# Six of eight batches' transposed activations kept whole and split later, and the transfer of the row maxima moved ahead of a store

## The chip, the cores and the metric

One Trainium2 chip, one of its cores. The metric is the device time of one execution in microseconds (us). The kernel is launched once; everything below happens inside that launch.

## What is computed

The input is `x`, 8 batches of 512 tokens of 256 numbers. After a layer norm over the 256 numbers (`xn`), three things are added:

    x + attention(xn) + moe(xn) + shared_mlp(xn)

- **Attention.** q, k and v come from low-rank projections (`xn @ basis.T`, 32 wide, then `@ (amp*cos(phase)).T`), 16 heads of 16; softmax over 512 keys; then another low-rank projection.
- **MoE.** Logits `xn @ gate_w.T` for 8 experts, softmax, the two best per token, and for these `silu(x@w_gate)*(x@w_up) @ w_down` with F = 352.
- **Shared MLP.** The same form with a hidden width of 704, for every token.

The kernel keeps float32 accuracy out of faster matmuls: an operand is split in a high part (rounded to the type the text below calls f32r) and a low part (the rest), and three products HI*HI, LO*HI, HI*LO are summed. A matmul of two whole float32 operands needs no split.

## The kernel before, in words

**Early part (to about 93 us).** VectorE (DVE) measures each batch (`measure`, L1660) and works out its scale (`scales`, L1672) with one square root on ScalarE (`root`, L870). ScalarE writes three quarters of the normed rows (`normal`, L875), GpSimd (POOL) one quarter. TensorE (PE) turns the rows (`turn_rows`, L1175), ScalarE copies the result rounded (`columns_high`, L884: two 128x512 copies) and DVE subtracts to get the low part (`columns_low`, L1721: two 128x512 subtractions). PE makes the logits (`logits`, L1184: four matmuls of 512 columns, high and low part of the activations against a gate whose 16 columns hold its own high and low part). The sync engine (SP) stores the rows for the experts' gather and both parts of the columns (`store_columns`, L482: 1 MB a batch) for the late part. Each engine runs its list in the order in which the code calls these helpers (ScalarE L897 to L918, PE L1201 to L1212, DVE L1731 to L1747). Routing follows on DVE from L1756.

**Middle part (93 to 367 us).** 71 tiles of 128 gathered tokens go through their experts (L1277 to L1341). Only the batch loads for the late part lie in it.

**Late part (367 to 950 us).** Batches are taken in reverse: batch b of this part is batch 7-b of the input (`of`, L398). Each batch has four slots g = 0 to 3, one per group of four heads, and each slot eight steps t = 0 to 7. In a step PE makes transposed scores (`score_T`), scores of a later group for the maxima (`score`), products with the values (`values`, float32 on both sides) and a piece of the shared MLP; ScalarE takes one exponential of 128x1024 (`exponent`, L1077), DVE one maximum of 128x1024 (L1872). The order on every engine is written out by hand (`slot` of ScalarE at L1109, of PE at L1600, of DVE at L1941, of SP at L662).

The maxima of group g+1 are made ready in slot g: DVE splits them at step 3 (`split_max`, L1874, two tiny operations from SBUF to SBUF), PE turns them at step 4 (L1383), ScalarE copies them at step 5 (`max_rows`, L1038), SP moves them into two rows of q (`load_max`, L631). The first `score_T` of the next slot waits for that transfer.

SP's other work in a slot: storing q's and k's parts of the next batch (`store_qk`, L620: three DMAs of 256 KB each, numbers 0 and 1 in slot 0, numbers 2 and 3 in slot 1), loading them back per group (`load_rows`, L548: four DMAs of 192 KB), moving the heads' sums and values (`move_sums` L637, `move_values` L643), and, for the heads of slots 2 and 3 of the batch before, storing the inverse sums (`store_inverse`, L651, in slot 0) and reading them back spread over the partitions (`load_inverse`, L656, in slot 1). POOL multiplies with these (`normalise`, L790), ScalarE rounds the product at step 4 of slot 1 (`ao_high`, L1092, L1095), ahead of `max_rows` in its list, POOL takes the low part (`ao_low`, L796), and PE uses both at step 7 of slot 1 (`low_rank_o`, L1551). `load_xT` (L585) brings the columns of batch b+2 (1 MB) in slot 2; PE's `low_rank(b+2)` (L1457) reads them at step 2 of slot 3.

## Time and profile before

| | us |
|---|---|
| median of 3 runs | 949.67 (949.47, 949.67, 953.66) |
| the profiled execution, its own time | 951.79 |
| its span in the profile | 950.0 |
| PE busy in the span | 864.2 (91%) |
| DVE busy | 612.4 (64%) |
| ScalarE busy | 574.5 (60%) |
| GpSimd busy | 410.4 (43%) |
| DMA moved | 140.04 MB |

A row of a timeline has a start, a duration, the engine, the line of the kernel, the operation, what it writes and reads, a count, and in brackets the idle time of that engine ahead of it with what ended it. PEld is the load of weights into PE. SPq rows are DMA issues: the duration is that of the issue and not of the transfer. A whole float32 matmul shows as two records.

### The profile page before, as it was taken

The numbers are of one execution on the slowest core, as the hardware profiler recorded it, in microseconds if no ns is written. First come the engines' busy times: TensorE is split into PE (matmuls) and PEld (weight loads), VectorE is DVE, ScalarE is ACT, GpSimd is POOL, SyncE is SP. The second block draws the span as 40 slices with busy tenths as digits, with TensorE's granted clock in tenths as the row PEclk, the third lists the DMA queues.
The fourth block names the chain that finished last, engine by engine and source line by source line (L and its number), as shares of the span: only waits on it lengthen the run. The fifth ranks groups of instructions, "written<-read, shape, count | busy, mean of one in ns | idle before, by whom it ended". The sixth has DMA issues, their size and how long they took to land.

```text
span 950.0 us, 19558 instructions
## 1 busy us (share of the span) xinstructions
PE 864.2 (91%) x6491; PEld 604.9 (64%) x6492; DVE 612.4 (64%) x923; ACT 574.5 (60%) x935; POOL 410.4 (43%) x411
## 2 busy tenths in 40 slices
PE   4755999999999989889989999999989999989995
PEld 2435999999999986456546555555546555555552
DVE  7787843434344455776776776776776786777752
ACT  5746744444444442766766866866756766767754
POOL 2003622222222151752762762753752763763841
PEclk9875999999999999989999999999999999999998
DMA  9994656222222216553863764754754865755410
GB/s 306 391 292 142 217 142 181 69 72 72 69 75 66 66 46 169 165 169 90 208 184 100 202 190 115 200 178 119 195 177 111 202 181 123 189 137 112 104 48 24
DMA packets 91480, 140.04 MB, mean 147 GB/s; under 512 B 17512, under 2 KB 51824, under 8 KB 89488
## 3 DMA queue, kind: packets, MB, share of 16 engines
q1 hardware_dynamic: 84720, 121.24, 44.7%
q0 software_dynamic: 6480, 17.70, 7.1%
q8 instruction: 44, 0.72, 0.3%
q14 instruction: 28, 0.23, 0.1%
q10 hardware_dynamic: 208, 0.14, 0.1%
HBM read 79.24 MB, written 54.71 MB: 141 GB/s over the span
## 4 chain that ended last, share of the span: by engine, by line
PE 68%; DVE 15%; DMA 6%; issue 4%; ACT 3%; SPq 2%; POOL 2%; DVEq 0%; ACTq 0%; POOLq 0%
PE s_pair L1295 8%; PE bank L1313 8%; PE bank L1453 8%; PE bank L1413 8%; PE bank L1517 7%; PE s_pair L1366 7%; PE st_pair L1295 6%; DVE top L1872 6%; PE st_pair L1441 5%; PE bank L1303 2%; PE bank L1278 2%; DMA q_rows<-top_T 1%; PE bank L1466 1%; DVE stats L1664 1%; PE bank L1426 1%
## 5 line engine op out<-in xcount | busy, mean ns | idle before, releaser
L1872 DVE TENSOR_REDUCE top<-s_pair 128x2 f32<-128x1024 f32 x248 | 303.7, 1224 | 139.6 <-PE s_pair L1366 138.2
L1083 ACT ACTIVATE prob<-st_pair 128x1024 f32<-128x1024 f32 x252 | 258.6, 1026 | 130.1 <-PE st_pair L1441 126.5
L756 POOL DMA_INDIRECT xg<-xn_rows,token_of x71 | 81.1, 1142 | 209.8 <-PE bank L1278 159.0
L1453 PE MATMUL bank<-prob,v_ones 128*32 128x512 f32 x1024 | 138.0, 611 | 2.2 <-ACT prob L1083 2.1
L1366 PE MATMUL s_pair<-k_rows,q_rows 48*128 48x512 f32 x496 | 113.4, 448 | 17.3 <-DVE top L1872 16.3
L1413 PE MATMUL bank<-xT_b,w_sh 64*128 64x512 f32 x960 | 128.8, 400 | 0.2
L1441 PE MATMUL st_pair<-q_rows,k_rows 50*128 50x512 f32 x504 | 105.5, 411 | 5.8 <-DMA q_rows<-top_T 3.0
L1413 PEld LDWEIGHTS bank<-xT_b,w_sh 64*128 64x128 f32 x960 | 90.3, 187 | 24.0 <-DVE h_f L1887 2.2
L1313 PE MATMUL bank<-w_exp,c_hT 128*128 (+1 forms) x639 | 94.2, 292 | 0.6 <-ACT c_y L995 0.6
L1366 PEld LDWEIGHTS s_pair<-k_rows,q_rows 48*128 48x128 f32 x496 | 48.1, 186 | 64.1 <-DVE top L1872 49.1
L1295 PE MATMUL s_pair<-w_exp,xg_T 128*128 x468 | 88.1, 338 | 0.0
L794 POOL TENSOR_TENSOR ao<-ao,o_sum 128x512 f32<-128x512 f32 x15 | 19.3, 1285 | 149.7 <-DMA o_sum<-inverse_rows 149.7
L1517 PEld LDWEIGHTS bank<-w_sh,h_T 64*128 64x128 f32 x1088 | 73.9, 189 | 12.5 <-issue 7.6
L1313 PEld LDWEIGHTS bank<-w_exp,c_hT 128*128 128x128 f32 (+1 forms) x639 | 81.1, 190 | 1.1 <-issue 1.1
L1517 PE MATMUL bank<-w_sh,h_T 64*128 64x256 f32 x1088 | 79.1, 286 | 2.4 <-DVE ro L1939 1.9
L778 POOL TENSOR_TENSOR h_f<-h_f,u_half 128x512 f32<-128x512 f32 x40 | 51.7, 1293 | 64.3 <-DVE h_f L1887 64.0
L1295 PEld LDWEIGHTS s_pair<-w_exp,xg_T 128*128 128x128 f32 x468 | 77.4, 195 | 0.3
L990 ACT ACTIVATE c_hT<-bank 128x384 fp32r<-128x384 f32 x71 | 34.9, 491 | 59.1 <-PE bank L1303 59.1
L1295 PE MATMUL st_pair<-w_exp,xg_T 128*128 x384 | 70.4, 332 | 0.0
L803 POOL DMA_INDIRECT y_b<-expert_rows,slot_of x64 | 63.8, 997 | 11.6 <-issue 6.6
L810 POOL TENSOR_SCALAR y_b<-y_b,share 128x256 f32<-128x256 f32 x64 | 58.4, 922 | 18.3 <-DMA y_b<-expert_rows,slot_of 18.2
L1844 DVE TENSOR_TENSOR xg_T<-bank,xg_T 128x256 fp32r<-128x256 f32 x71 | 30.1, 424 | 55.4 <-ACT xg_T L980 55.4
(230 smaller groups left out, 1229.0 us busy)
## 6 DMA issues: line engine op xcount, KB each, us to landing
qk_rows<-qk_hi SPq DMA_DIRECT2D x56, 256.0 KB
q_rows<-qk_rows SPq DMA_DIRECT2D x64, 192.0 KB
k_rows<-qk_rows SPq DMA_DIRECT2D x56, 192.0 KB
expert_rows<-c_y SPq DMA_DIRECT2D x71, 128.0 KB, 1.7
xn_T_split<-x_T SPq DMA_DIRECT2D x8, 1024.0 KB, 6.5
xT_b<-xn_T_split SPq DMA_DIRECT2D x7, 1024.0 KB, 8.7
qk_rows<-qk_lo SPq DMA_DIRECT2D x28, 256.0 KB
x_all<-in_L_attn_x_dram SPq DMA_DIRECT2D x8, 512.0 KB, 8.2
```

The source lines that it names most:

```text
L756: pool.indirect_dma_start(xg[s % 4][:, :], None, xn_dram, bass.IndirectOffsetOnAxis(token_of[:, s:s + 1], 0)).then_inc(c_x[s % 4], 16)
L803: pool.indirect_dma_start(y_b[:, t % 2, k, :], None, y_dram, bass.IndirectOffsetOnAxis(slot_of[:, k, of(b) * TPB + t:of(b) * TPB + t + 1], ...
L810: pool.tensor_scalar(y_b[:, t % 2, k, :], y_b[:, t % 2, k, :], share[:, of(b) * TPB + t, k:k + 1], None, ALU.mult).then_inc(p_ys, 1)
L1083: act.activation(prob[n % 3][:, 2 * jp:2 * jp + 2, :].rearrange("p j l -> p (j l)"), score_T_pair(b, g, t)[:, :], ACT.Exp, scale=HD ** -0. ...
L1295: ins = pe.matmul(gu_bank_of(s, i)[n][:, 0:F], xg_T[i % 2][:, a * KT + k, :], w, start=(m == 0 and k == 0), stop=(m == 2 and k == KT - 1))
L1313: ins = pe.matmul(y_bank[:, 0:D], c_hT[i % 2][0:n, a, k, :], w, start=(m == 0 and k == 0), stop=(m == 2 and k == FT - 1))
L1366: ins = pe.matmul(score_pair(b, g, v)[:, i * 512:(i + 1) * 512], q_rows[g][r:r + 48, jp, qt * P:(qt + 1) * P], k_rows[g][r:r + 48, jp, :], ...
L1413: ins = pe.matmul((g_bank, u_bank)[up][:, :], w_sh[rows, a, o:o + P], xT_of(b)[rows, c, k, :], start=(n == 0 and i == 0), stop=(n == 1 and ...
L1441: ins = pe.matmul(score_T_pair(b, g, t)[:, i * 512:(i + 1) * 512], k_rows[g][r:r + QK_ROWS, jp, kt * P:(kt + 1) * P], q_rows[g][r:r + QK_R ...
L1453: ins = pe.matmul(ot_bank[32 * j:32 * j + 32, :], v_ones[:, kt, 4 * g + j, :], prob[(b * 16 + g * 4 + kt) % 3][:, j, :], start=(kt == 0), ...
L1517: ins = pe.matmul((g_bank, u_bank)[to][:, 0:D], h_T[rows, a, f, t * P:(t + 1) * P], w_sh[rows, c, S_GU + f * D:S_GU + (f + 1) * D], start= ...
L1872: dve.tensor_reduce(top[g % 2][:, :, jp, qt], score_pair(b, g, v)[:, :].rearrange("p (i k) -> p i k", i=2), AX_X, ALU.max).then_inc(d_max, 1)
```

## The change

1. Batches 0 to 5 of the input (`in_parts` false) are kept as whole float32 columns: ScalarE's two copies write float32, DVE's two subtractions are left out, PE makes the logits with two float32 matmuls instead of four, and SP stores 512 KB instead of 1 MB. PE's `turn_rows` waits for the copy of two batches before, no longer for its subtraction. DVE adds one memset and two copies of 128x8 for a float32 gate.
2. In the late part `load_xT` reads 512 KB for these batches (b = 2 to 7 there). ScalarE makes the high part in one copy of 128x1024 (`columns_out`, slot 2, step 6), POOL the low part in one subtraction of 128x1024 (`columns_rest`, ahead of `last_group`). PE waits for POOL's `p_xl`.
3. In SP's list of a slot `load_max` is ahead of `store_qk` 0 and 2, and `load_xT` is behind `load_inverse`, `move_sums` and `move_values`.
4. Two semaphores are merged into others (`rows_ok` into `hot_ok`, `d_iv` into `d_to`), with the same waits.

```diff
@@ SP
+        WHOLE = NB - 2
+        def in_parts(b):
+            return b >= WHOLE
...
             def store_columns(b):
                 wait(sp, xt_hi, b + 1)
-                wait(sp, xt_lo, b + 1)
+                if not in_parts(b):
+                    sp.dma_start(xT_dram[b][:, 0:KT * L],
+                                 x_W[b % NXT][:, HI, :, :].rearrange("p k l -> p (k l)")).then_inc(xT_stored[b % NXT], 16)
+                    return
+                wait(sp, xt_lo, b - WHOLE + 1)
...
             def load_xT(b):
                 if b >= 2:
                     wait(sp, b_gu, (b - 1) * SFT)
+                if in_parts(of(b)):
...
+                else:
+                    sp.dma_start(xT_of(b)[:, LO, :, :].rearrange("p k l -> p (k l)").bitcast(F32), xT_dram[of(b)][:, 0:KT * L]).then_inc(xT_in, 16)
...
             def slot(b, g):
-                if g == 2 and there(b + 2):
-                    load_xT(b + 2)
                 if ppg % 2 and moved(ppb, ppg // 2):
                     load_inverse(ppb, ppg // 2)
                 if pg % 2 and moved(pb, pg // 2):
                     move_sums(pb, pg)
                     move_values(pb, pg)
-                if g == 0 and there(b + 1):
-                    store_qk(b + 1, 0)
-                if g == 1 and there(b + 1):
-                    store_qk(b + 1, 2)
+                if g == 2 and there(b + 2):
+                    load_xT(b + 2)
                 if g == 2 and there(b - 1):
                     store_out(b - 1, 0)
                 if g == 3 and there(b + 2):
                     store_low_rank(b + 2)
                 if there(nb):
                     load_max(nb, ng)
+                if g == 0 and there(b + 1):
+                    store_qk(b + 1, 0)
+                if g == 1 and there(b + 1):
+                    store_qk(b + 1, 2)
@@ GpSimd
+            def columns_rest(b):
+                wait(pool, a_xh, b - 1)
+                lo = xT_of(b)[:, LO, :, :].rearrange("p k l -> p (k l)")
+                pool.tensor_tensor(lo, lo.bitcast(F32), xT_of(b)[:, HI, :, :].rearrange("p k l -> p (k l)").bitcast(F32),
+                                   ALU.subtract).then_inc(p_xl, 1)
...
                 sum_y(b, 3)
+                if there(b + 2):
+                    columns_rest(b + 2)
                 last_group(b)
@@ ScalarE
-                    ins = act.activation(x_T[b % NXT][:, HI, k, :], xt_bank[b % 2][k][:, :], ACT.Copy)
+                    ins = act.activation((x_T if in_parts(b) else x_W)[b % NXT][:, HI, k, :], xt_bank[b % 2][k][:, :], ACT.Copy)
...
+            def columns_out(b):
+                wait(act, xT_in, b * 16)
+                act.activation(xT_of(b)[:, HI, :, :].rearrange("p k l -> p (k l)"),
+                               xT_of(b)[:, LO, :, :].rearrange("p k l -> p (k l)").bitcast(F32), ACT.Copy).then_inc(a_xh, 1)
...
+                    if g == 2 and t == 6 and there(b + 2):
+                        columns_out(b + 2)
@@ TensorE
-                wait(pe, xt_lo, b - 1)
+                wait(pe, xt_hi, b - 1)
...
             def logits(b):
-                wait(pe, xt_lo, b + 1)
                 wait(pe, lg_kept, b)
+                if not in_parts(b):
+                    wait(pe, xt_hi, b + 1)
+                    for k in range(KT):
+                        ins = pe.matmul(lgT_bank[0:2 * NE, :], gate_F[:, k, :, :].rearrange("p c e -> p (c e)"), x_W[b % NXT][:, HI, k, :],
+                                        start=(k == 0), stop=(k == KT - 1))
+                    ins.then_inc(lg_turned, 1)
+                    return
+                wait(pe, xt_lo, b - WHOLE + 1)
...
             def low_rank(b):
-                wait(pe, xT_in, b * 16)
+                wait(pe, xT_in, 16) if b == 1 else wait(pe, p_xl, b - 1)
@@ VectorE
             small_parts()
-            columns_low(0)
             scales(2)
             for b in range(3, 7):
                 measure(b)
-                columns_low(b - 2)
                 scales(b)
-            columns_low(5)
             angles()
-            columns_low(6)
-            columns_low(7)
+            for b in range(WHOLE, NB):
+                columns_low(b)
             thrice()
```

## Rows read from the trace of the kernel before

**Rows 1.** Busy time by engine, granted clock and DMA, of the late part.

```profile
core 0: us, PE busy (x) PEld busy (x) DVE busy (x) ACT busy (x) POOL busy (x), PEclk, DMA share, GB/s
...
367.40:950.00 582.60, 545.11 (x4395) 310.50 (x4395) 412.09 (x487) 390.32 (x532) 310.12 (x302) 0.98 0.56 147
```

**Rows 2.** Waits by releaser: us in total, times, longest.

```profile
PEld st_pair L1441 <- DMA q_rows<-top_T: 6.6, 6, 2.2
...
PE st_pair L1441 <- DMA q_rows<-top_T: 3.0, 2, 1.7
```

**Rows 3.** Chain that ended last, early part: start, us, what.

```profile
15.30 1.17 DVE x_T L1724 x2
...
32.83 1.19 DVE x_T L1724 x2
...
46.31 0.70 DVE lg L1756
```

**Rows 4.** Timeline of ScalarE, early part.

```profile
25.72 1.57 ACT L881 ACTIVATE x_n<-x_all,rs 128x256 f32<-128x256 f32 x3
...
29.44 1.57 ACT L881 ACTIVATE x_n<-x_all,rs 128x256 f32<-128x256 f32 x3
...
34.96 1.58 ACT L881 ACTIVATE x_n<-x_all,rs 128x256 f32<-128x256 f32 x3 [0.92 <-DVE rs L1679]
```

**Rows 5.** Timeline of PE, early part: the logits of two batches.

```profile
34.07 1.89 PE L1190 MATMUL bank<-x_T,gate_T 128*16 128x512 f32 x4 [1.56 <-DVE x_T L1724]
...
41.84 1.11 PE L1190 MATMUL bank<-x_T,gate_T 128*16 128x512 f32 x4
```

**Rows 6.** Timeline of PE, end of slot 1 of batch b = 3.

```profile
621.19 0.40 PE L1441 MATMUL st_pair<-q_rows,k_rows 50*128 50x512 f32 x2
621.52 1.06 PE L1453 MATMUL bank<-prob,v_ones 128*32 128x512 f32 x8
...
626.95 0.50 PE L1441 MATMUL st_pair<-q_rows,k_rows 50*128 50x512 f32 x2 [1.69 <-DMA q_rows<-top_T]
...
627.75 1.93 PE L1453 MATMUL bank<-prob,v_ones 128*32 128x512 f32 x8
```

**Rows 7.** Busy time by engine of five batch periods, columns as in rows 1.

```profile
651.52:724.05 72.53, 68.76 (x554) 39.14 (x550) 54.03 (x63) 48.63 (x68) 38.62 (x38) 0.98 0.60 161
724.05:793.74 69.69, 67.15 (x554) 38.33 (x550) 52.92 (x63) 49.16 (x68) 39.95 (x39) 1.00 0.64 168
sum 354.06, PE 339.07 PEld 193.23 DVE 263.58 ACT 244.57 POOL 195.79; mean PE 67.81 PEld 38.65 DVE 52.72 ACT 48.91 POOL 39.16
```

**Rows 8.** Timeline of SP, slots 0 and 1 of batch b = 3.

```profile
599.14 1.36 SPq L627 DMA_DIRECT2D qk_rows<-qk_hi  x2
...
606.40 0.35 SPq L654 DMA_DIRECT2D inverse_rows<-o_inv  x1
...
611.11 0.62 SPq L660 DMA_DIRECT2D o_sum<-inverse_rows  x1
...
619.45 1.82 SPq L634 DMA_DIRECT2D q_rows<-top_T  x2
```

**Rows 9.** Timeline of GpSimd, slots 2 and 3 of b = 2, slot 1 of b = 3.

```profile
579.84 1.28 POOL L794 TENSOR_TENSOR ao<-ao,o_sum 128x512 f32<-128x512 f32 x1 [17.09 <-DMA o_sum<-inverse_rows]
...
616.87 1.29 POOL L794 TENSOR_TENSOR ao<-ao,o_sum 128x512 f32<-128x512 f32 x1 [0.28 <-DMA o_sum<-inverse_rows]
```

**Rows 10.** Timeline of ScalarE, slot 1 of batch b = 3.

```profile
618.65 0.65 ACT L1095 ACTIVATE ao_T<-ao 128x512 fp32r<-128x512 f32 x1
...
619.38 1.03 ACT L1083 ACTIVATE prob<-st_pair 128x1024 f32<-128x1024 f32 x1
```

**Rows 11.** Timeline of ScalarE, step 7 of slot 2 of batch b = 2.

```profile
573.50 1.02 ACT L1083 ACTIVATE prob<-st_pair 128x1024 f32<-128x1024 f32 x1 [1.61 <-PE st_pair L1441]
```

**Rows 12.** Single lines of code: durations in ns, least, median, most; last row: landing of load_xT.

```profile
L764 POOL TENSOR_TENSOR w_sh<-raw_all,w_sh x4: 2494/2520/2547, 338.2 to 351.8; 128x1088 fp32r<-128x1088 f32 x4
...
L1881 DVE TENSOR_TENSOR top_parts<-top,top_parts x32: 174/176/1345, 366.4 to 916.4; 128x16 fp32r<-128x16 f32 x32
...
DMA to landing us min/median/max: 5.4/8.7/9.0
```

More of the change, by code:

```diff
@@ L137, in build_program @@
         gate_T = sb("gate_T", [P, KT, 2, NE], F32R, region)
+        gate_F = sb("gate_F", [P, KT, 2, NE], F32, region)
         stats = sb("stats", [P, NT, 6], F32, region)
@@ L201, in build_program @@
         tail.close()
+        whole = ExitStack()
+        sb("first_experts_w", [P, NE - 5, 2, W_ALL], F32R, whole)
+        sb("fourth_w", [P, 2 * W_ALL], F32R, whole)
+        sb("fifth_w", [P, 2 * W_ALL], F32R, whole)
+        x_W3 = sb("x_W3", [P, 2, KT, L], F32, whole)
+        sb("rest_of_sixth_w", [P, 2 * W_ALL - 2 * KT * L], F32R, whole)
+        sb("x_n_w", [P, 2, TPB, D], F32, whole)
+        x_W = [sb(f"x_W{i}", [P, 2, KT, L], F32, whole) for i in range(3)] + [x_W3]
+        whole.close()
         e_hi += [x_T[0][:, HI, k, :] for k in range(KT)]
@@ L275, in build_program @@
         xT_stored = [sem(f"xT_stored{i}") for i in range(NXT)]
-        angle_ok, thrice_ok, rows_hi, rows_ok, norm_ok = (sem(n) for n in ("angle_ok", "thrice_ok", "rows_hi", "rows_ok", "norm_ok"))
+        angle_ok, thrice_ok, rows_hi, norm_ok = (sem(n) for n in ("angle_ok", "thrice_ok", "rows_hi", "norm_ok"))
         xt_ps = sem("xt_ps")
@@ L289, in build_program @@
         a_done = sem("a_done")
+        a_xh, p_xl = sem("a_xh"), sem("p_xl")
         c_x = [sem(f"c_x{i}") for i in range(4)]
@@ L340, in build_program @@
             sem(f"d_{n}") for n in ("r", "qk", "max", "mh", "m", "ga", "hb", "inv", "res", "dn", "po"))
-        b_to, b_bo, d_iv, d_to, a_bo, d_bo = (sem(n) for n in ("b_to", "b_bo", "d_iv", "d_to", "a_bo", "d_bo"))
+        b_to, b_bo, d_to, a_bo, d_bo = (sem(n) for n in ("b_to", "b_bo", "d_to", "a_bo", "d_bo"))
         d_hl = sem("d_hl")
@@ L1259, in _ @@
             pe.matmul(bank[1][:, 0:NT * NE], ones_b[:, :], hb, start=True, stop=True).then_inc(count_ps, 1)
-            pe.wait_ge(rows_ok, 1)
+            pe.wait_ge(hot_ok, 2)
             for n in range(3):
@@ L1399, in gate_up_shared @@
                     if q == 0:
-                        wait(pe, xT_in, b * 16) if b else wait(pe, xF_in, 64)
+                        if b >= 2:
+                            wait(pe, p_xl, b - 1)
+                        else:
+                            wait(pe, xT_in, 16) if b else wait(pe, xF_in, 64)
                         wait(pe, d_dn, b * TPB)
@@ L1544, in low_rank_o @@
                     wait(pe, p_ao, 2 * b + 1)
-                    pe.wait_ge(d_to, 1)
+                    pe.wait_ge(d_to, 2)
                 else:
@@ L1563, in turn_back @@
             def turn_back(h):
-                wait(pe, d_to, h + 1)
+                wait(pe, d_to, 2 * h + 2)
                 wait(pe, d_po, LAST * 2)
@@ L1691, in small_parts @@
             def small_parts():
+                st.did(dve.memset(gate_F[:, :, LO, :], 0.0))
                 dve.wait_ge(pe_prep, 1)
@@ L1698, in small_parts @@
                     st.did(dve.tensor_copy(basis_T[:, k, HI, 3:6, :], o))
+                    st.did(dve.tensor_copy(gate_F[:, k, HI, :], g))
                     st.then(dve.tensor_copy(gate_T[:, k, HI, :], g))
@@ L1718, in small_rows @@
                                             w_rows[32:64, 2 * i:2 * i + 2, :].rearrange("p n d -> p (n d)").bitcast(F32), ALU.subtract)
[L1719 removed]
+                ins.then_inc(hot_ok, 1)
             def columns_low(b):
@@ L1925, in share_last_o @@
                 wait(dve, inv_st, (2 * LAST + 1) * 16)
-                dve.reciprocal(inv, turned_o(h)[:, :, :, HD:HD + 1]).then_inc(d_iv, 1)
-                wait(dve, d_iv, h + 1)
+                dve.reciprocal(inv, turned_o(h)[:, :, :, HD:HD + 1]).then_inc(d_to, 1)
+                wait(dve, d_to, 2 * h + 1)
                 wait(dve, p_nm, 2 * LAST + 1)
```

3 lines of the change are left out of this document (1 added, 2 removed).

## The prediction, made before the changed kernel was built or run

> **What bounds the kernel now.** I read the busy shares by stage first, then the waits by releaser, then the chain that ended last, and at the end the timelines where a wait recurs. PE is busy for 545.11 of the late part's 582.60 us [rows 1], so there only a gap on PE can be won back. One such gap belongs to the change: the first transposed scores of a slot wait for the transfer of the maxima, 3.0 us on PE in two places and 6.6 us on its weight loads in six [rows 2]. In the early part PE is not the bound. The chain runs on DVE and passes through its subtractions for the low parts, five pairs of which lie on it, the first at 15.30, the last at 32.83, 1.2 us each [rows 3]. The middle part is not touched.
>
> The five batch periods that lie wholly in the late part sum to 354.06 us, 70.81 on average; the shortest is 69.69 and the longest 72.53 [rows 7]. The shortest still does all the work, so what the others have above it, 1.1 us on average, is stall that can go.
>
> **Early part, DVE's subtractions gone.** By DVE's own list the five pairs would give 5 x 1.19 = 5.9 us. I don't take that, because ScalarE is about as late. Its normed rows start at 25.72 and 29.44, 3.72 apart, without a wait for DVE [rows 4]; that loop (turn on PE, copy, normal) stays as long as it was. Only the last one, at 34.96, waits for DVE (0.92 us), after the double measurement of batches 6 and 7 [rows 4]. By my step through the lists DVE would be done with that at 33.5 instead of 34.94, since its start hangs on ScalarE's root and not on its own list. So 1.3 us come from there. DVE's added memset and two tiny copies (some 0.1 us each, estimated from operations of that size) are inside that slack.
>
> **Early part, logits.** Four matmuls take 1.11 us at the higher clock and 1.89 at the lower [rows 5]. The price of a whole float32 matmul of 512 columns I take from the products with the values: eight records, two to a matmul, four matmuls side by side in the array, so two records one after the other, take 1.06 us [rows 6], and 1.93 when PE had just waited 1.69 us and ran at the lower of its two levels [rows 6]. Two such matmuls one after the other are 2.1 or 3.9 us: 1.0 to 2.0 us more on PE for each of six batches. PE has room for it in the loop of 3.72 us (transposes 1.1, small ones 0.4, logits 2.1: 3.6, just so) if the clock is up; at the lower clock it is 6.4 and PE would be the bound. PE did run at the lower level at 34.07, after a wait of 1.56 [rows 5]; with longer matmuls and shorter waits I expect the upper level there, which gives back another 0.5 us before the routing starts at 46.31 [rows 3]. Sum for the early part: -1.8 us, bounds -5.9 (DVE's list alone) and +3 (two batches' logits at the lower clock on the chain, 2 x 1.9, less some 0.8 won on DVE).
>
> 3 MB less are stored (6 x 0.5). Nobody on the chain waits for these stores, so they are counted at nothing; if they were what hides, the gain would be larger and not smaller.
>
> **Late part, the split.** ScalarE gains one copy of 128x1024, about 1.05 us (as an exponential of the same size, 1.02 [rows 11]), after the exponential of step 6 in slot 2. ScalarE then idles 1.61 us ahead of step 7's [rows 11], so it costs nothing if the data are there. They should be: load_xT is moved behind the five moves of sums and values and is delayed by another 2.0 us of issues in slot 1, to about 565.4 in batch 2 against 559.05; 1 MB took 8.7 us to land [rows 12], half of it should take about 6, so 571.5, and the copy would start at 571.9. That is tight. Bounds: 0, and 1 us in each of six batches. I take 0, as the row before step 7 has room for a copy that is half a microsecond late.
>
> POOL gains a subtraction of 128x1024; 128x1088 took 2.52 [rows 12], so 2.4 us. POOL idles 17.09 us there, until 579.84 [rows 9], and PE's low_rank wants it at 580.5: started at 573.0 it is done at 575.4. Cost nothing, cover 5 us. This subtraction has a second price. The two tiny operations that split the maxima take 0.18 us as a rule, but one of 32 took 1.345 [rows 12], in the longest period [rows 7], beside a POOL multiplication from SBUF. The Trainium skill, page "SBUF — State Buffer", section "SBUF: two separate sides", says that POOL and DVE share a pair of ports with an exclusive lock, so that the later one is blocked for the whole instruction. This trace agrees, with that 1.345; by the rule a subtraction of 2.4 us that met DVE's split would cost up to 2.2 us, which is rival 3. In the order as written the split is at step 3 and the subtraction after step 6, so I take 0.
>
> **Late part, SP's order.** The maxima are issued when ScalarE has copied them, at 619.45 [rows 8], and land for PE at 626.95, after 1.69 us of PE idle [rows 6]; ahead of them in the queue lie 768 KB of store_qk. At the late part's rate (147 GB/s at a DMA share of 0.56 [rows 1], so about 262 at full share) these are 3.0 us of transfer. Without them the maxima land some 3 us earlier and PE doesn't wait. Besides, PE runs at the lower level after such a wait (1.93 against 1.06 [rows 6]), another 0.9. So a stalled batch falls back to the shortest period. Batch 0 has the same gap in its slot 1 and no inverse sums to wait for: -1.3.
>
> What is late next: the three stores of q's part (1.36 for two [rows 8], so 2.0 us) now stand ahead of load_rows, store_inverse and store_qk 1. store_inverse, at 606.40, is issued some 1.7 to 2.0 later, and load_inverse, which waits for its landing (611.11 [rows 8]), with it. The product on POOL at 616.87 already waits 0.28 for that [rows 9]. It ends at 618.16, and ScalarE takes it at 618.65 [rows 10], so the first 0.5 us are free. The exponential behind it ends at 620.41 [rows 10], PE wants it at 621.19 [rows 6], so another 0.8 are free. If o_sum is later by X, PE stalls by X - 1.25. X has the bounds 0 (the same bytes in front of it in the end) and 5.0 (2.0 of issue and the 3.0 of transfer). I take 1.9, nearest to the delay of the issue: 0.65 us for each of six batches. The lateness at low_rank_o behind it should vanish in the wait of PE for DVE that follows.
>
> So a period becomes 69.7 + 0.65 = 70.35, 0.46 less than the mean before, times five: -2.3. The sixth batch: -0.5. Batch 0: -1.3. Late part: -4.1.
>
> **The sum.** -1.8 - 4.1 = -5.9 us. The profiled execution took 951.79 by its own time (span 950.0), so it would take 945.9; it stands 2.1 above the median of 949.67, and the median would be 943.8. Half a percent is 4.75 us, about what a measurement of this kernel can tell from no change.
>
> **Rivals.**
> 1. *Hidden anyway* (chance 0.20). PE's float32 logits at the lower clock take the early gain, and the end of a stalled slot is held by DVE's maxima a moment later than by the transfer, as it is in the periods without that stall. For it: the 69.69 period has no gap for the maxima and still isn't free of others. Against: the period of 70.99 with the 1.69 gap is just 1.3 longer. Then only batch 0 gains something, -0.7: 949.0.
> 2. *The inverse sums turn into the new wait* (0.14), the case on the other side. Place: ScalarE's copy of the product at step 4 of slot 1, in front of the maxima's copy and an exponential. Its price is X - 1.25 in six batches. Against 1.1 of stall that goes and the 3.6 us won elsewhere (0.6 a batch) it decides from X = 2.95. With X = 4.0, six times (2.75 - 1.1) = +9.9, less 1.3 and 1.8: +6.8, 956.5. For it: no slack on the POOL product. Against: the bytes ahead are the same in sum, and store_qk 1 will be nearly done when load_inverse is issued.
> 3. *The half megabyte lands late* (0.06). ScalarE then stands in front of step 7, POOL's subtraction slides towards the split of the maxima and can lock DVE. 1.5 us in six batches, +9.0 on the forecast: 952.8, up to 958 if the lock is met each time.
>
> **Numbers.** Forecast 0.60, own range 940 to 947, three quarters of it below 944.9; rivals 0.20, 0.14, 0.06. Faster by over half a percent: 0.45. Within: 0.15 from the forecast, 0.20 from rival 1, 0.04 from the lower ends of 2 and 3: 0.39. Slower: 0.16. The range of 8 in 10 goes from 939 (the forecast with a larger share of DVE's 5.9) to 955 (short of rival 2's value).
>
> **What would show it.** Right: routing (L1756) starts near 44.5; ScalarE's normed rows still 3.7 apart; no wait of L1441 for the maxima; ScalarE's L1095 idle by about 1.4 ahead of it; POOL's L794 in slot 1 with a wait near 2; periods near 70.3. Wrong: logits of 3.9 us in the early part; periods above 71.5 with ScalarE waiting at L1095; an idle of ScalarE ahead of columns_out; L1879 or L1881 blocked in several batches.

## The result, and the profile after

The changed kernel takes 981.68 us (median of four runs, 976.1 to 982.18) against 949.57 for the kernel before, measured beside it: a ratio of 1.032, interval 1.027 to 1.037. It is 32 us slower. The forecast was 943.8, the range ended at 955, and slower had a chance of 0.16. The profiled execution took 981.74 by its own time, with a span of 979.9. One run of e10 (979.13 us) and one of the kernel before beside e1 to e4 (961.94) fell in a slower state of the chip and are left out of the ratios.

Line numbers after the change: L818 is the product (`normalise`), L1132 ScalarE's rounding of it (`ao_high`), L1490 `score_T`, L1120 the exponential, L1412 the scores for the maxima, L1600 `low_rank_o`, L1920 DVE's maxima, L684 and L678 the load and the store of the inverse sums, L658 the maxima's transfer, L651 and L653 `store_qk`, L579 `load_rows`.

The late part, and the batch periods, from the busy time by engine (stretch, length, busy time and instructions of each engine, granted clock, DMA share, GB/s):

```profile
364.78:979.90 615.12, 563.42 (x4395) 316.16 (x4395) 410.06 (x487) 396.30 (x538) 323.16 (x308) 0.95 0.50 134
...
437.18:512.93 75.75, 70.42 (x555) 39.38 (x551) 52.48 (x63) 49.88 (x69) 41.65 (x40) 0.95 0.55 147
512.93:589.27 76.34, 71.65 (x555) 39.82 (x551) 52.00 (x63) 50.05 (x69) 41.15 (x40) 0.93 0.53 146
...
sum 378.64, PE 353.15 PEld 197.87 DVE 261.56 ACT 249.68 POOL 206.49; mean PE 70.63 PEld 39.57 DVE 52.31 ACT 49.94 POOL 41.30
```

The late part starts 2.6 us earlier than before [rows 1] and takes 32.5 us more. A period that was 70.8 on average [rows 7] is 75.7, and the granted clock, 0.98 to 1.00 before, is 0.93 to 0.95. The instructions are the same in number.

Waits by releaser (us in total, times, longest):

```profile
PEld st_pair L1490 <- ACT prob L1120: 27.5, 28, 4.9
...
ACT ao_T L1132 <- POOL ao L818: 25.9, 6, 5.7
PE st_pair L1490 <- ACT prob L1120: 23.3, 8, 4.6
```

The wait for the maxima's transfer [rows 2] is gone. In its place ScalarE waits 25.9 us in six batches for the product on POOL, which it never did before, and PE waits for ScalarE. The issues of the sync engine (SP), slots 0 and 1 of b = 3, to be laid beside [rows 8]:

```profile
611.44 1.40 SPq L658 DMA_DIRECT2D q_rows<-top_T  x2
612.95 1.32 SPq L651 DMA_DIRECT2D qk_rows<-qk_hi  x2
614.31 0.57 SPq L653 DMA_DIRECT2D qk_rows<-qk_lo  x1
614.99 2.58 SPq L579 DMA_DIRECT2D k_rows<-qk_rows  x2
617.61 1.02 SPq L579 DMA_DIRECT2D q_rows<-qk_rows  x2
618.73 0.38 SPq L678 DMA_DIRECT2D inverse_rows<-o_inv  x1
619.22 1.21 SPq L651 DMA_DIRECT2D qk_rows<-qk_hi  x2
...
624.56 0.65 SPq L684 DMA_DIRECT2D o_sum<-inverse_rows  x1
```

And two issues of the kernel before that [rows 8] leave out, between the maxima's and the store of the inverse sums:

```profile
604.23 0.80 SPq L558 DMA_DIRECT2D k_rows<-qk_rows  x2
605.06 0.91 SPq L558 DMA_DIRECT2D q_rows<-qk_rows  x2
```

POOL, ScalarE and PE behind it, from three timelines (start, us, what, in brackets the idle time ahead and its releaser; before: [rows 9], [rows 10], [rows 6]):

```profile
630.74 1.26 POOL L818 TENSOR_TENSOR ao<-ao,o_sum 128x512 f32<-128x512 f32 x1 [6.91 <-DMA o_sum<-inverse_rows]
...
632.04 0.63 ACT L1132 ACTIVATE ao_T<-ao 128x512 fp32r<-128x512 f32 x1 [4.05 <-POOL ao L818]
...
632.73 1.00 ACT L1120 ACTIVATE prob<-st_pair 128x1024 f32<-128x1024 f32 x1
...
633.78 0.49 PE L1490 MATMUL st_pair<-q_rows,k_rows 50*128 50x512 f32 x2 [3.23 <-ACT prob L1120]
634.20 1.09 PE L1502 MATMUL bank<-prob,v_ones 128*32 128x512 f32 x8
635.22 0.80 PE L1402 MATMUL bank<-r_rows,w_rows 96*128 96x512 f32 x1
...
637.10 2.87 PE L1600 MATMUL bank<-ao_T,basis_T 128*96 128x512 f32 x6
...
641.05 1.48 PE L1502 MATMUL bank<-prob,v_ones 128*32 128x512 f32 x8
```

The load of the inverse sums is issued 13.1 us behind the maxima of slot 0; before it was 8.4 (602.72 to 611.11 in the same list). The product starts 19.3 us behind them instead of 14.1. ScalarE, whose list has the rounding first, keeps the maxima's copy and the next exponential back, PE idles 3.23 us, and for some 7 us behind that its matmuls are long: 2.87 us for the six of L1600 that took 1.64 before, at the lower of the clock's two levels.

Where the DMA engines were meanwhile shows best in stretches of 4 us counted from the issue of the maxima (602.72 before, 611.44 after). Before:

```profile
596.72:600.72 4.00, 4.00 (x33) 2.07 (x29) 2.97 (x5) 3.20 (x5) 2.41 (x3) 1.00 1.10 234
600.72:604.72 4.00, 3.81 (x31) 2.06 (x29) 3.66 (x5) 3.00 (x5) 3.69 (x5) 1.00 0.61 190
604.72:608.72 4.00, 4.00 (x33) 2.11 (x29) 2.98 (x3) 3.14 (x5) 2.85 (x4) 1.00 0.96 254
608.72:612.72 4.00, 4.00 (x34) 2.42 (x32) 3.11 (x4) 3.72 (x7) 3.84 (x5) 1.00 0.66 191
612.72:616.72 4.00, 4.00 (x33) 2.22 (x31) 2.75 (x5) 3.19 (x5) 3.55 (x4) 1.00 0.49 173
```

After:

```profile
605.44:609.44 4.00, 4.00 (x33) 2.07 (x29) 2.96 (x4) 3.19 (x5) 2.90 (x4) 1.00 1.05 236
609.44:613.44 4.00, 3.34 (x28) 1.62 (x27) 4.00 (x6) 3.00 (x5) 3.73 (x5) 1.00 0.05 13
613.44:617.44 4.00, 4.00 (x33) 2.17 (x29) 2.63 (x4) 2.65 (x4) 3.71 (x5) 1.00 0.57 157
617.44:621.44 4.00, 4.00 (x34) 2.35 (x32) 3.44 (x4) 3.72 (x6) 3.75 (x5) 1.00 0.92 240
621.44:625.44 4.00, 4.00 (x33) 2.15 (x31) 2.51 (x3) 3.19 (x5) 2.23 (x2) 1.00 0.61 205
```

In the second stretch the DMA engines moved 190 GB/s before and 13 after, a difference of 177 x 4.00 = 708 KB, nearly the 768 KB of q's store. SP's last issue before the maxima ended at 607.39, and then it stood at them until 611.44. The data of q's store were ready meanwhile, the high part (512 KB) from 607.79 on and the low part (256 KB) from 610.37 on, from the timelines of ScalarE and DVE:

```profile
607.19 0.60 ACT L1068 ACTIVATE qk_hi<-bank 128x512 fp32r<-128x512 f32 x1 [0.33 <-PE bank L1402]
...
609.69 0.68 DVE L1913 TENSOR_TENSOR qk_lo<-bank,qk_hi 128x512 fp32r<-128x512 f32 x1
```

SP stood, and the DMA engines stood too. In the third stretch they are behind once more (157 GB/s against 254). In the fourth and fifth, where the inverse sums have to pass, they move more than before (240 and 205 against 191 and 173).

The early part, timelines of PE and ScalarE (before: [rows 5], [rows 4]):

```profile
23.26 1.89 PE L1229 MATMUL bank<-x_W,gate_F 128*16 128x512 f32 x4
...
26.99 1.89 PE L1229 MATMUL bank<-x_W,gate_F 128*16 128x512 f32 x4
...
23.99 1.58 ACT L913 ACTIVATE x_n<-x_all,rs 128x256 f32<-128x256 f32 x3
...
27.72 1.57 ACT L913 ACTIVATE x_n<-x_all,rs 128x256 f32<-128x256 f32 x3
```

The chain that ended last has the start of the routing (before: [rows 3]):

```profile
42.68 0.70 DVE lg L1804
```

It is 3.6 us earlier. One of these comes back at the start of the middle part, where PE waits 2.33 us for the fourth tile's gather; before it waited 0.50 there.

### The profile page after: what moved, and what is told of

Its sections match the earlier page's. It is cut to its first block, busy times and chain, and to the rows that moved or that the text cites. A ratio compares the mean times of both kernels' runs of the same rounds, so it can differ in the third digit from the quotient of the medians.

```text
span 979.9 us, 19555 instructions
## 1 busy us (share of the span) xinstructions
PE 882.6 (90%) x6491; PEld 607.7 (62%) x6492; DVE 604.6 (62%) x914; ACT 580.4 (59%) x941; POOL 424.0 (43%) x417
## 4 chain that ended last, share of the span: by engine, by line
PE 64%; DVE 11%; DMA 9%; ACT 5%; issue 5%; SPq 4%; POOL 2%; ACTq 0%; DVEq 0%; POOLq 0%
PE bank L1359 8%; PE s_pair L1341 7%; PE bank L1566 7%; PE bank L1502 7%; PE st_pair L1341 6%; PE bank L1462 6%; PE s_pair L1412 5%; DVE top L1920 5%; PE st_pair L1490 5%; DMA o_sum<-inverse_rows 3%; DMA inverse_rows<-o_inv 3%; PE bank L1349 2%; PE bank L1600 2%; SPq L579 2%; PE bank L1324 2%
## 5 line engine op out<-in xcount | busy, mean ns | idle before, releaser
L1920 DVE TENSOR_REDUCE top<-s_pair 128x2 f32<-128x1024 f32 x248 | 303.8, 1225 | 172.5 <-PE s_pair L1412 164.3
L1120 ACT ACTIVATE prob<-st_pair 128x1024 f32<-128x1024 f32 x252 | 258.5, 1026 | 127.9 <-PE st_pair L1490 118.0
L1502 PE MATMUL bank<-prob,v_ones 128*32 128x512 f32 x1024 | 141.7, 627 | 2.2 <-ACT prob L1120 2.1
L1490 PE MATMUL st_pair<-q_rows,k_rows 50*128 50x512 f32 x504 | 109.1, 425 | 23.3 <-ACT prob L1120 23.3
L1412 PE MATMUL s_pair<-k_rows,q_rows 48*128 48x512 f32 x496 | 115.4, 457 | 13.7 <-DVE top L1920 12.4
L1412 PEld LDWEIGHTS s_pair<-k_rows,q_rows 48*128 48x128 f32 x496 | 49.1, 191 | 62.0 <-DVE top L1920 45.7
L1566 PEld LDWEIGHTS bank<-w_sh,h_T 64*128 64x128 f32 x1088 | 73.7, 188 | 14.7 <-issue 9.7
L1490 PEld LDWEIGHTS st_pair<-q_rows,k_rows 50*128 50x128 f32 x504 | 50.6, 193 | 40.9 <-ACT prob L1120 27.5
L818 POOL TENSOR_TENSOR ao<-ao,o_sum 128x512 f32<-128x512 f32 x15 | 19.1, 1276 | 104.6 <-DMA o_sum<-inverse_rows 104.6
```

The lines of the kernel that those rows point to most:

```text
L1120: act.activation(prob[n % 3][:, 2 * jp:2 * jp + 2, :].rearrange("p j l -> p (j l)"), score_T_pair(b, g, t)[:, :], ACT.Exp, scale=HD ** -0. ...
L1412: ins = pe.matmul(score_pair(b, g, v)[:, i * 512:(i + 1) * 512], q_rows[g][r:r + 48, jp, qt * P:(qt + 1) * P], k_rows[g][r:r + 48, jp, :], ...
L1490: ins = pe.matmul(score_T_pair(b, g, t)[:, i * 512:(i + 1) * 512], k_rows[g][r:r + QK_ROWS, jp, kt * P:(kt + 1) * P], q_rows[g][r:r + QK_R ...
L1502: ins = pe.matmul(ot_bank[32 * j:32 * j + 32, :], v_ones[:, kt, 4 * g + j, :], prob[(b * 16 + g * 4 + kt) % 3][:, j, :], start=(kt == 0), ...
L1566: ins = pe.matmul((g_bank, u_bank)[to][:, 0:D], h_T[rows, a, f, t * P:(t + 1) * P], w_sh[rows, c, S_GU + f * D:S_GU + (f + 1) * D], start= ...
L1920: dve.tensor_reduce(top[g % 2][:, :, jp, qt], score_pair(b, g, v)[:, :].rearrange("p (i k) -> p i k", i=2), AX_X, ALU.max).then_inc(d_max, 1)
```

## The experiments

Three theories stood at first: **A**, the late inverse sums, behind the store of q's part; **B**, the split in the late part; **C**, in e1 to e4, is the new order of slot 1. A' (from e5 on) is A with the bytes between the maxima and the load of the inverse sums in the place of the store's position. From e8 on the letter C stands for the theory of volume, A' carried further: what counts is how much the DMA engines still have to move there. The groups of runs e1 to e4, e5 to e7, e8 to e10 and e11 and e12 each have their own runs of the kernel before beside them (950.13, 949.37, 950.12 and 948.48 us), so two medians of different groups compare to a us or two; the ratios are safer. All kernels compute the whole output.

**e1, the stores first again.** `store_qk` 0 and 2 back ahead of `load_max`; split and `load_xT` as changed.

```diff
+                if g == 0 and there(b + 1):
+                    store_qk(b + 1, 0)
+                if g == 1 and there(b + 1):
+                    store_qk(b + 1, 2)
                 if there(nb):
                     load_max(nb, ng)
-                if g == 0 and there(b + 1):
...
```

> The changed kernel with the maxima's transfer put back behind the stores of q's parts in slots 0 and 1; all else as changed. Theory A (the late inverse sums: in slot 0 the store of q's part now stands ahead of the rows' loads and of the store of the inverse sums, the product on GpSimd comes late, ScalarE waits for it in front of the maxima's copy, PE stalls and falls to its lower clock): 944 to 949 us, ScalarE's waits ahead of L1132 (25.9 us in the changed kernel) gone. Theory B (the split in the late part and the moved load of the columns cost the time): still 975 or more. Theory C (slot 1's new order is at fault) can't be told from A here: 944 to 949.

Measured: 945.31 us (10 runs), ratio 0.996 (0.993 to 0.999). The whole loss goes. Five periods of it:

```profile
sum 350.09, PE 336.33 PEld 191.99 DVE 262.54 ACT 249.44 POOL 209.09; mean PE 67.27 PEld 38.40 DVE 52.51 ACT 49.89 POOL 41.82
```

The changed kernel's five take 28.6 us more, 5.7 a batch. PE's busy time for the same work is 353.15 against 336.33, so 3.4 of the 5.7 us a batch are matmuls that run longer and 2.3 are idle time.

**e2, the kernel before with that order alone.** Only `load_max` ahead of `store_qk` 0 and 2.

```diff
@@ the kernel before
+                if there(nb):
+                    load_max(nb, ng)
                 if g == 0 and there(b + 1):
                     store_qk(b + 1, 0)
...
```

> The kernel before with nothing changed but the place of the maxima's transfer, ahead of the stores of q's parts in slots 0 and 1. Theory A: slower by about what the changed kernel lost plus what its early part won, 977 to 985 us, with ScalarE waiting at L1095 for 4 us in each of six batches. Theory B: 948 to 951. Theory C: as A.

Measured: 982.87 us (4 runs), ratio 1.034 (1.028 to 1.041). The order alone makes the loss, and B (the split) has no part in it.

**e3, slot 1 only.** The changed kernel with `store_qk` 0 back ahead of the maxima, number 2 still behind them.

```diff
+                if g == 0 and there(b + 1):
+                    store_qk(b + 1, 0)
                 if there(nb):
                     load_max(nb, ng)
-                if g == 0 and there(b + 1):
-                    store_qk(b + 1, 0)
```

> The changed kernel with the maxima ahead of the store in slot 1 alone; in slot 0 the store is back ahead of them. Theory A: no late inverse sums, and the maxima are early where PE had waited for them: 940 to 946 us, 2 to 5 below the run with both stores first. Theory C: 970 or more. Theory B: 975 or more.

Measured: 946.43 us (10 runs), ratio 0.996 (0.993 to 0.999). The loss comes from slot 0. In slot 1, where the maxima's transfer was the wait to be removed, the wait is gone and nothing is gained (mean of the six periods 70.73, against 70.18 in e1 and 70.67 in e7). The theory's second half, 2 to 5 us below e1, was a miss: it is 1.1 above. PE idles at that place for DVE's maximum,

```profile
626.61 0.50 PE L1412 MATMUL s_pair<-k_rows,q_rows 48*128 48x512 f32 x2 [1.02 <-DVE top L1920]
```

In e1, with the store still ahead of the maxima, PE has the same 1.02 us for DVE's maximum in three of the six slots, and itself waits for the transfer once, 0.36 us. So there was next to nothing to gain.

**e4, the store of the inverse sums early.** `store_inverse` right behind `load_max` in the changed kernel.

```diff
                 if there(nb):
                     load_max(nb, ng)
+                if pg % 2 and moved(pb, pg // 2):
+                    store_inverse(pb, pg // 2)
...
-                if pg % 2 and moved(pb, pg // 2):
-                    store_inverse(pb, pg // 2)
```

> The changed kernel with the store of the inverse sums right behind the maxima's transfer, ahead of the store of q's part and of the rows' loads. Theory A: the sums are on their way some 6 us earlier, the product on GpSimd is no longer late and the whole loss is gone: 938 to 945 us, ScalarE's waits ahead of its copy of the product under 1 us a batch. Theories B and C: 972 or more.

Measured: 989.82 us (4 runs), ratio 1.041 (1.035 to 1.048). A miss. The store goes out 5.8 us sooner (2.0 behind the maxima instead of 7.8, means over the six batches), and yet the product is later:

```profile
634.40 1.26 POOL L818 TENSOR_TENSOR ao<-ao,o_sum 128x512 f32<-128x512 f32 x1 [7.11 <-DMA o_sum<-inverse_rows]
```

That is 19.8 us behind the maxima (614.56); in the changed kernel it was 19.3. So the place of the store in SP's list isn't what decides, and A fell in that form. A' put the backlog of bytes in its place.

**e5, the inverse sums' round trip ahead of the rows.** Slot 0: maxima, `store_inverse`, `store_qk` 0 and 1, `load_inverse`, `load_rows`.

```diff
                 if there(nb):
                     load_max(nb, ng)
+                if g == 0 and moved(b - 1, 1):
+                    store_inverse(b - 1, 1)
                 if g == 0 and there(b + 1):
                     store_qk(b + 1, 0)
...
+                if g == 0 and there(b + 1):
+                    store_qk(b + 1, 1)
+                if g == 0 and moved(b - 1, 1):
+                    load_inverse(b - 1, 1)
```

> The changed kernel with slot 0 of SP in the order maxima, store_inverse, store_qk 0, store_qk 1, load_inverse, load_rows (slots 1 to 3 as changed). Nothing is left out. Theory A' (what decides is how much lies in SP's list and queue between the maxima and load_inverse): load_inverse is issued 7.1 us behind the maxima's issue instead of 13.1 (10.4 in the kernel where only store_inverse was early), POOL's product comes out 2 us before ScalarE wants it, ScalarE waits for it 0 to 3 us in all, periods of 69.7 to 70.7, 938 to 945 us. Rival E (any order with the maxima ahead of the stores delays the same bytes, and the loss only moves to k's part or to the rows of the next group): above 965 us, with the waits of e4 or new ones for k_rows. Rival B (the split in the late part): 975 us or more.

Measured: 1006.92 us (6 runs), ratio 1.060 (1.057 to 1.063). The worst of all; A' missed here, and rival E was right.

```profile
629.74 1.45 SPq L684 DMA_DIRECT2D o_sum<-inverse_rows  x1
631.30 2.60 SPq L579 DMA_DIRECT2D k_rows<-qk_rows  x2
634.26 1.76 SPq L579 DMA_DIRECT2D q_rows<-qk_rows  x2
...
641.66 1.26 POOL L822 TENSOR_TENSOR ao<-ao,o_sum 128x512 f32<-128x512 f32 x1 [7.55 <-DMA o_sum<-inverse_rows]
...
643.74 0.79 PE L1416 MATMUL s_pair<-k_rows,q_rows 48*128 48x512 f32 x2 [7.31 <-DMA q_rows<-qk_rows]
```

`load_inverse` is issued 8.0 us behind the maxima (621.70), as early as in the kernel before, and lands 11.9 us later instead of 5.8: 1.5 MB issued just ahead of it and 768 KB just behind share the engines with it. Then the rows are late too, and PE waits 7.31 us for them. A' was right to look at the bytes and wrong to count only those in front.

**e6, the rounding two steps later.** ScalarE's `ao_high` of slot 1 behind the exponential of step 6, SP as changed.

```diff
-                    if t == 4 and g % 2 and moved(ppb, ppg // 2):
+                    if t == 6 and g == 1 and moved(ppb, ppg // 2):
+                        ao_high(ppb, ppg // 2)
+                    if t == 4 and g == 3 and moved(ppb, ppg // 2):
                         ao_high(ppb, ppg // 2)
```

> The changed kernel, SP's order untouched; ScalarE's rounding of the product in slot 1 stands behind the exponential of step 6 instead of that of step 4. Nothing is left out. Theory A' (the late inverse sums cost what they cost because the rounding stands ahead of the maxima's copy and two exponentials in ScalarE's list): the product still comes 5 us late, but ScalarE's wait falls from about 4.3 to 0 to 1.5 us a batch, PE has no stall of 3 us or more at that place, periods of 70 to 72.5, 945 to 960 us. Rival F (the late product hurts by another way, the low part and the PE's low_rank_o behind it): PE waits there instead, periods stay above 74, 970 us or more.

Measured: 977.51 us (4 runs), ratio 1.031 (1.026 to 1.035). Rival F: ScalarE's order is only where the delay comes through first. Without it PE waits as long for the low part (25.4 us in all, against 23.3 for ScalarE in the changed kernel), which POOL makes behind the product, with three other instructions between them:

```profile
632.97 2.88 PE L1602 MATMUL bank<-ao_T,basis_T 128*96 128x512 f32 x6 [4.78 <-POOL ao_T L822]
```

**e7, the split alone.** SP's order of the late part wholly as before.

```diff
+                if g == 2 and there(b + 2):
+                    load_xT(b + 2)
                 if ppg % 2 and moved(ppb, ppg // 2):
                     load_inverse(ppb, ppg // 2)
...
```

> The changed kernel with SP's order of the late part all as before (stores of q's parts ahead of the maxima, load_xT first in slot 2): only the split is left of the change. Against the kernel before it shows the split alone, against the run with the stores first what load_xT's place is worth. Theory: the place is worth nothing, 943 to 948 us, with the late part's start near 364.5 and periods of 70.2 on average. Rival G (the place behind the moves is what made the periods 0.7 us shorter): 948 to 951 us, periods of 70.9. Rival H (three quarters of the late gain are the half megabyte less per load): as the theory, not told apart here.

Measured: 947.5 us (12 runs), ratio 0.997 (0.995 to 0.999), as the theory said. It isn't told apart from e1 (0.996). The late part starts at 365.70 in its profile; over the twelve profiles with the split the mean is 364.8, over the two without it 367.6. So the split gives 2.8 us in the early part and nothing that can be seen in the late part.

**e8, other bytes into the gap.** The changed kernel; `load_rows` of slot 0 ahead of the maxima, q's store still behind them.

```diff
+                if there(rb) and g == 0:
+                    load_rows(rb, rg)
                 if there(nb):
                     load_max(nb, ng)
...
-                if there(rb):
+                if there(rb) and g:
                     load_rows(rb, rg)
```

> The changed kernel with one thing moved: in slot 0 of SP the load of a later group's rows (768 KB) is issued ahead of the maxima instead of behind them. The maxima stay ahead of q's store. Nothing is left out. Theory C (volume: before the change q's store filled DMA time that is now idle, shares 0.39 and 0.34 in 608 to 616, and the bytes have moved in front of, beside and behind the load of the inverse sums, shares 0.81 and 0.76 in 616 to 624; which 768 KB fill that time doesn't matter): load_inverse is issued about 8.5 us behind the maxima's issue instead of 13.1, POOL's product is back to a wait below 2 us, no 3 us stall of PE, periods of 69.7 to 70.8, 940 to 948 us. Rival E (what costs is the maxima ahead of q's store, wherever the rows are): the loss stays, 970 us or more. Between them, 950 to 965, both have a part.

Measured: 954.09 us (12 runs), ratio 1.004 (1.002 to 1.007), in the range in which both have a part. The theory missed with its time and with POOL's wait (3.2 to 4.2 us in five of six batches, not below 2), and was right that no PE stall of 3 us is left (the longest wait of the transposed scores for ScalarE is 1.53). The rows fill the gap (4 us around the maxima's issue):

```profile
600.15:604.15 4.00, 3.81 (x31) 2.05 (x29) 3.66 (x5) 3.00 (x5) 3.69 (x5) 1.00 1.02 195
```

and 28 of 32 us of the loss are gone with the maxima still ahead of q's store. What stays is 4 us against the kernel before, or 9 against e1 (8 by the ratios). Two things show in its trace: from the issue of the load to the product it takes 0.9 us more than in e1, and the wait of ScalarE is 1.3 us a batch.

**e9, rows and q's store both ahead of the maxima.**

```diff
+                if there(rb) and g == 0:
+                    load_rows(rb, rg)
+                if g == 0 and there(b + 1):
+                    store_qk(b + 1, 0)
...
                 if there(nb):
                     load_max(nb, ng)
```

> The same, and q's stores of slots 0 and 1 ahead of the maxima as before the change: slot 0 is rows, q's store, maxima, store_inverse, k's store. A candidate for the best of all. Theory C: the inverse sums have less in front of them than in any order so far, but nothing waited for them in e1 (945.31 us) any more, so the gain over it is 0 to 2 us: 942 to 946 us. Rival: 1.5 MB ahead of the maxima delay them so that the first transposed scores wait for them in slot 0 too, 1 to 3 us a batch: 949 to 960 us.

Measured: 961.9 us (6 runs), ratio 1.014 (1.009 to 1.019). The rival, 2 us above its range: now the maxima are what is late, once in each of six batches. The waits by releaser:

```profile
PEld st_pair L1492 <- DMA q_rows<-top_T: 11.7, 6, 2.8
PE st_pair L1492 <- DMA q_rows<-top_T: 9.1, 6, 2.4
```

**e10, a third of the dose.** The changed kernel with q's high parts (512 KB) ahead of the maxima and the low part (256 KB) behind.

```diff
+                if g == 0 and there(b + 1):
+                    store_qk(b + 1, 0, (0,))
                 if there(nb):
                     load_max(nb, ng)
                 if g == 0 and there(b + 1):
-                    store_qk(b + 1, 0)
+                    store_qk(b + 1, 0, (1,))
```

> The changed kernel with two thirds of q's store of slot 0 (its high parts, 512 KB) put back ahead of the maxima; only the low part (256 KB) stays behind them. Nothing is left out. A dose of a third. Theory C with a threshold: the product on POOL comes 1.3 to 2.0 us late instead of 5, less 1.25 that is free, so 0 to 0.8 us of stall a batch, periods of 70.2 to 71.5, 944 to 951 us. Rival K (no slack: any lateness is paid in full and twice, by the lower clock after the stall): a third of the loss, 955 to 960 us.

Measured: 948.33 us (12 runs), ratio 0.999 (0.997 to 1.001). A third of the bytes costs a tenth of the loss or less (3.0 of 36.4 us, against e1). Whether that is a threshold isn't shown, because the third wasn't a neutral one: the low part was ready only 1.1 us before the maxima were issued, the high part 3.7 us before (the changed kernel, b = 3). With the high parts ahead of them, the DMA share in the 4 us around the maxima's issue is 0.44 to 0.49 in the six batches, not far from the kernel before (0.46 to 0.61). The product is 0.9 us later than before, and PE's stall in b = 3 is

```profile
620.17 0.50 PE L1493 MATMUL st_pair<-q_rows,k_rows 50*128 50x512 f32 x2 [0.23 <-ACT prob L1123]
```

**e11, a queue of their own.** SP's order as changed; both transfers of these inverse sums issued by ScalarE.

```diff
@@ ScalarE's slot
+                    if (g, t) == (0, 6) and moved(b - 1, 1):
+                        store_inverse(b - 1, 1)
+                    if (g, t) == (1, 1) and moved(b - 1, 1):
+                        load_inverse(b - 1, 1)
```

> The changed kernel, SP's order otherwise untouched; the two transfers of slots 2 and 3's inverse sums (store_inverse in slot 0, load_inverse in slot 1) are issued by ScalarE, behind its exponentials of step 6 and of step 1, and so have a queue of their own. Nothing is left out. Theory C1 (the lateness is that of SP's queue: the order of its list and the bytes it has outstanding): the store goes out 3 us earlier and both land in about the 4.7 and 5.5 us of the kernel before or less; POOL's product waits no longer than before, ScalarE's wait for it is below 1 us, periods of 69.7 to 71.0, 940 to 948 us, less the 0.2 to 0.6 us a batch that the issue costs on ScalarE. Rival C2 (the lateness is that of the 16 DMA engines, which all queues share: 1.5 MB in the same 8 us): both transfers take as long as in the changed kernel or longer, ScalarE waits 1 to 3 us a batch, 955 to 970 us.

Measured: 969.63 us (6 runs), ratio 1.023 (1.020 to 1.027): C2. The load is issued 9.3 us behind the maxima (604.67), as before the change, and takes until 623.16:

```profile
607.71 0.32 ACTq L897 DMA_DIRECT2D inverse_rows<-o_inv  x1
...
613.93 0.60 ACTq L903 DMA_DIRECT2D o_sum<-inverse_rows  x1
...
623.16 1.27 POOL L818 TENSOR_TENSOR ao<-ao,o_sum 128x512 f32<-128x512 f32 x1 [6.27 <-DMA o_sum<-inverse_rows]
```

With SP's list out of the way the transfer alone takes 9.2 us instead of 5.8. The Trainium skill, page "DMA: Bandwidth & Descriptors", section "Issuing engines are not separate DMA queues", says that transfers issued by different engines run on the same 16 DMA engines and interleave. The trace agrees, with these 9.2 us.

**e12, the same with the stores first.** e1 with e11's two moves.

```diff
@@ e11
+                if g == 0 and there(b + 1):
+                    store_qk(b + 1, 0)
+                if g == 1 and there(b + 1):
+                    store_qk(b + 1, 2)
                 if there(nb):
                     load_max(nb, ng)
...
```

> The same with q's stores of slots 0 and 1 ahead of the maxima as before the change (e1 with the inverse sums by ScalarE's queue). A candidate for the best. Theory: in e1 (945.31 us) nothing waited for the inverse sums, so their own queue gains nothing and ScalarE's issues cost 0 to 0.5 us a batch: 944 to 949 us. Rival: SP's queue without them gets the maxima through sooner, 942 to 944 us.

Measured: 949.49 us (12 runs), ratio 1.000 (0.998 to 1.002), half a us above the theory's range. The second queue gains nothing over e1 (0.996).

**What decides.** Means in us over the six batches, each read from the timelines of SP (in e11 ScalarE), POOL and ScalarE: the issue of the load behind that of slot 0's maxima, from there to the product, their sum, ScalarE's wait, the batch period, and the median.

| kernel | issue | transfer | product | wait | period | us |
|---|---|---|---|---|---|---|
| before | 9.3 | 5.7 | 15.0 | 0 | 71.1 | 949.6 |
| e1 | 9.2 | 5.8 | 15.0 | 0.2 | 70.2 | 945.3 |
| e3 | 9.4 | 6.0 | 15.4 | 0 | 70.7 | 946.4 |
| e10 | 10.1 | 5.8 | 15.9 | 0.7 | 70.9 | 948.3 |
| e8 | 9.7 | 6.6 | 16.4 | 1.3 | 71.2 | 954.1 |
| e11 | 9.3 | 8.7 | 18.0 | 2.9 | 73.8 | 969.6 |
| e2 | 13.3 | 5.7 | 19.0 | 4.1 | 75.3 | 982.9 |
| after | 13.6 | 5.8 | 19.4 | 4.3 | 75.2 | 981.7 |
| e4 | 10.8 | 9.8 | 20.5 | 5.0 | 76.7 | 989.8 |

Four orders in which the DMA engines idle around the maxima's issue (e11, e2, after, e4) put issue and transfer together in very different ways and all have the product at 18 to 20.5 us. The five at the top, with bytes in that gap, have it by 16.4 at the latest. (e5, also without bytes there, has it at 18.5, with waits for the rows on top, and e6 at 19.2; e7 and e12 have it at 15.3 and 14.7. e9 has it at 14.5 and is slow by the maxima alone.) The DMA share in the 4 us around the maxima's issue parts the same two groups in every batch: 0.03 to 0.20 in e11, e2, after, e4, e5 and e6, and 0.44 or more in all others. What is read as "issued too late" in one order is "transferred too slowly" in the next. The reading that fits all of them is that the sum follows the moment when the DMA engines start on the 2.3 MB of the slot; that is argued from these means, and e8 is the run made to show it.

## Why the prediction was wrong

**The step that failed** is X, the lateness of the inverse sums: "X has the bounds 0 ... and 5.0 (2.0 of issue and the 3.0 of transfer). I take 1.9, nearest to the delay of the issue". It is 4.4 us (19.4 less 15.0), near the upper bound, and all of it in the issue: the load goes out 4.4 us later (13.6 less 9.3), and from there to the product nothing changes (5.8 and 5.7). For the store of the sums "some 1.7 to 2.0" were counted, and it goes out 4.1 later (7.8 less 3.6). In b = 3 X is 5.2: 3.6 until the store's issue, 1.1 until the store has landed and 0.4 in the load. Of the 3.6, 2.0 are the issues of q's store, just as counted. The 1.8 that were not counted are k's rows (issued in 2.58 us, before in 0.80); from q's rows on, 0.2 come back. The value of 1.9 was the time of q's issues alone, and the lower bound stood on the same bytes being ahead in the end. They are, but before they were moved in time in which nobody else needed the DMA engines. The text costed what q's store would be in front of, and never what would fill its old place. SP's wait for the maxima was put in front of a store that was ready.

**The price of a stall** failed as well. "PE stalls by X - 1.25" would be 3.15 us; less the 1.1 of stall counted as gone that is +2.05 in six batches, and with the other terms 959 us. The clock was used on the side of the gain alone (0.9 us for the wait that goes), not on that of the cost. Against e1 a batch costs 2.3 us of idle time and 3.4 us of longer matmuls. 6 x 3.4 = 20 us is most of what lies between 959 and 982, and three quarters of the 27 by which the range missed.

**The maxima's transfer** was to give 1.3 us per stalled batch. It gives nothing that can be measured (e3 against e1). This is rival 1's mechanism: DVE's maximum comes a moment later, and PE idles 1.02 us for it where it idled 1.69 for the transfer [rows 6].

**Right, with their sizes.** The early part: predicted -1.8, measured -3.6 at the routing and -2.8 at the start of the late part. ScalarE's loop stayed at 3.73 us; the float32 logits took 1.89 us for two matmuls against my 2.1, and PE stayed at the higher level, as I had said (granted clock 1.00 from 20 to 44 us; before 0.68 and 0.50 in 32 to 40). The larger gain is on the side of DVE's list, whose bound was 5.9. The split in the late part at nothing: ScalarE's copy 1.05 us and POOL's subtraction 2.39, as estimated, the half megabyte in 4.4 us against my 6, no wait behind them, and of rival 3 nothing (the two splits of the maxima, L1927 and L1929, took over 0.5 us in five of 64 cases, none beside the subtraction). The next in line was named rightly, with its place (ScalarE's rounding ahead of the maxima's copy) and its sign: rival 2 is what happened. It had 0.14 and a value of 956.5, for want of the two sizes above. With X at its measured 4.4 us, inside its own bounds, and the clock counted, that rival's value comes to 959 + 20 = 979, reckoned afterwards.

Rightly left out: the semaphores; e1, e3 and e7 have them merged and lose nothing. Not shown: what makes up e8's 9 us above e1, since the bytes of q's store in front of the load of the sums, the slower issues and the order of the rows changed together; and why e12's first period was 75.0.

**A version ahead of both.** e1 and e3 (0.996, both intervals below 1) are 0.4% faster than the kernel before, e7 (0.997) 0.3%, and all are some 3.5% faster than the changed one: the split, with q's store of slot 0 ahead of the maxima. That is a small gain, and the three aren't told apart.

## What to carry to other kernels

Before a wait is moved forward in an in-order DMA list, look at the DMA engines' share at that place. If it is high (0.61 here) and the wait ends late, the transfers behind it were filling time that nobody else wants, and the engines will stand idle (0.05 here); the bytes then meet the next urgent transfer, and neither an earlier place in the list (e4, e5) nor a queue of its own (e11, a third of the loss back) saved that one. Cost a long stall on TensorE at its idle time and the slower matmuls behind it as well: here 2.3 us a batch came with 3.4.

## What the runs showed of the hardware

- The issue of a DMA isn't of fixed length. Two issues of 192 KB took 0.80 us in the kernel before, 2.58 after, 3.35 in e11; that of 16 KB took 0.35 and in e8 1.46; that of the inverse sums 0.62 and in e5 1.45. These long ones stand behind 768 KB or more issued back to back. Such bytes ahead don't make every issue long: the 0.35 us in the kernel before [rows 8] came behind the 768 KB of rows.
- From the issue of a 256 KB load (the inverse sums) to the product that waited for it took 5.2 us to 11.9 us in slot 1, by what was issued around it, also behind it (e5); in slot 3 of the kernel before it was 3.7 to 4.3.
- In e5, where PE idled 7.31 us until 643.74, the granted clock was 0.56 in the 4 us inside that stall and 0.50 in the 4 us in which it ended:

```profile
638.00:642.00 4.00, 0.00 (x0) 0.00 (x0) 0.00 (x0) 0.28 (x1) 0.34 (x1) 0.56 0.56 155
642.00:646.00 4.00, 2.26 (x10) 0.48 (x10) 1.43 (x2) 0.63 (x1) 3.20 (x3) 0.50 0.16 53
```

- After 3.23 us of idle time in the changed kernel the first eight matmuls still ran at the higher level (1.09 us at 634.20, granted clock 1.00), and those from 636 to 641 at the lower (0.50): the cost of a stall appears behind it, and no wait shows it.
